# A GNN and FFN stack on one core: the products of the zero matrix in TensorE's waits are taken out

## The reference

```python
edge_index = jnp.stack([src, dst])                        # 8192 edges
x = x + L0_gnn(layernorm(x), edge_index, ...)             # GAT, 8 heads of 768, then GAT with one head
x = x + L0_ffn(layernorm(x)[None], ...)[0]                # class tokens, 5 atoms, gates
x = x + L1_gnn(layernorm(x), ..., edge_index)             # the same GAT again
x = x + L1_ffn(layernorm(x)[None], ...)[0]                # 768 -> 512 -> 768 -> 768
x = x + L2_gnn(layernorm(x), edge_index, W, b)            # GCN
x = x + L2_ffn(layernorm(x)[None], ...)[0]                # 8 experts of 64, the best one
x = x + L3_gnn(layernorm(x), edge_index, edge_type, ...)  # 34 relations, then GCN
x = x + L3_ffn(layernorm(x)[None], ...)[0]                # 8 experts of 96, the best two, layer norm
```

## Time and profile before

| | |
|---|---|
| median of three runs | 1344.08 us |
| the profiled execution's own time | 1338.48 us |
| its span, first to last instruction | 1336.7 us |
| TensorE busy | 1272.1 us, 95% |
| TensorE's weight loads busy | 1131.4 us, 85% |
| VectorE busy | 994.8 us, 74% |
| ScalarE busy | 643.2 us, 48% |
| mean granted clock of TensorE | 0.995 |

### The profile page before, as it was taken

How to read it: one execution, slowest core, us unless ns; L and a number is a source line. 1 busy time by engine, 2 the same in 40 slices (tenths; PEclk the granted TensorE clock), 3 DMA queues, 4 the chain that set the end, 5 groups by cost and what they waited for, 6 DMA issues and landing times.

```text
span 1336.7 us, 20982 instructions
## 1 busy us (share of the span) xinstructions
PE 1272.1 (95%) x7760; PEld 1131.4 (85%) x7778; DVE 994.8 (74%) x1639; ACT 643.2 (48%) x835; POOL 198.3 (15%) x160
## 2 busy tenths in 40 slices
PE   6999999988899999988898999999999999999997
PEld 4788999965888999967677889888888988888886
DVE  6998888987798888986867666655666665566676
ACT  5666566545566566545345433333443333343342
POOL 0023443430024443430000000000000000000200
PEclk9999999999999999999999999999999999999999
DMA  9495666654445666544245444554444454443640
GB/s 336 161 269 174 180 208 201 176 145 125 147 172 173 186 208 195 182 117 143 87 166 184 177 157 168 190 186 162 157 157 159 185 185 177 157 157 142 203 119 31
DMA packets 103929, 227.40 MB, mean 170 GB/s; under 512 B 16759, under 2 KB 34999, under 8 KB 103889
## 3 DMA queue, kind: packets, MB, share of 16 engines
q1 hardware_dynamic: 72972, 192.43, 40.6%
q10 hardware_dynamic: 20980, 31.78, 8.5%
q0 software_dynamic: 9936, 2.66, 2.2%
HBM read 216.56 MB, written 10.29 MB: 170 GB/s over the span
## 4 chain that ended last, share of the span: by engine, by line
PE 79%; DVE 12%; ACT 3%; DMA 3%; issue 2%; DVEq 0%; ACTq 0%; SPq 0%
PE bank L445 78%; DVE w_lo L1369 3%; DMA w_in<-L_gnn_W 2%; ACT w_hi L1011 1%; DVE stats L1407 1%; PE bank L541 1%; DVE h_lo L1369 1%; PE bank L484 1%; DMA w_in<-L_gnn_W_root 1%; DMA x_sb<-x 1%; DVE neg_b L1372 0%; DVE hid_lo L1369 0%; DVE x_sb L1369 0%; DVE xT_lo L1369 0%; DVE scores_b L1375 0%
## 5 line engine op out<-in xcount | busy, mean ns | idle before, releaser
L1011 ACT ACTIVATE w_hi<-w_in 128x2304 fp32r<-128x2304 f32 (+4 forms) x162 | 328.9, 2063 | 233.2 <-PE bank L445 198.7
L1369 DVE TENSOR_TENSOR w_lo<-w_in,w_hi 128x2304 fp32r<-128x2304 f32 (+4 forms) x162 | 396.6, 2477 | 58.3 <-ACT w_hi L1011 58.2
L445 PE MATMUL bank<-w_hi,xT_hi 128*128 128x384 f32 (+3 forms) x942 | 322.9, 343 | 6.2 <-DVE xT_lo L1369 4.2
L445 PE MATMUL bank<-w_lo,xT_hi 128*128 128x384 f32 (+3 forms) x942 | 306.2, 337 | 0.0
L445 PE MATMUL bank<-w_hi,hid_hi 128*128 128x512 f32 (+3 forms) x858 | 293.8, 342 | 7.6 <-DVE hid_lo L1369 4.4
L445 PE MATMUL bank<-w_lo,hid_hi 128*128 128x512 f32 (+3 forms) x858 | 271.3, 337 | 0.0
L445 PE MATMUL bank<-w_hi,xT_lo 128*128 128x384 f32 (+3 forms) x942 | 244.9, 338 | 0.0
L445 PE MATMUL bank<-w_hi,hid_lo 128*128 128x512 f32 (+3 forms) x858 | 224.9, 338 | 0.0
L445 PEld LDWEIGHTS bank<-w_hi,xT_hi 128*128 128x128 f32 (+1 forms) x942 | 176.4, 187 | 32.6 <-issue 5.7
L445 PEld LDWEIGHTS bank<-w_hi,hid_hi 128*128 128x128 f32 (+1 forms) x858 | 161.5, 188 | 44.5 <-issue 5.9
L1945 DVE SCALAR_TENSOR_TENSOR neg_b<-bank,rinv,neg_b 128x512 f32<-128x512 f32 (+1 forms) x136 | 77.4, 611 | 153.3 <-PE bank L445 153.3
(11 more groups left out here) (253 smaller groups left out, 1509.4 us busy)
## 6 DMA issues: line engine op xcount, KB each, us to landing
w_in<-L_gnn_W_rel SPq DMA_DIRECT2D x68, 1152.0 KB, 5.6
w_in<-L_gnn_W SPq DMA_DIRECT2D x66, 1152.0 KB, 5.7
table<-zrow SPq DMA_DIRECT2D x4, 2304.0 KB, 16.4
scores_b<-table ACTq DMA_DIRECT2D x34, 256.0 KB, 2.9
a_bc<-L_gnn_a_src ACTq DMA_DIRECT2D x18, 384.0 KB, 3.8
a_bc<-L_gnn_a_dst ACTq DMA_DIRECT2D x18, 384.0 KB, 5.3
key_row<-key_rows ACTq DMA_DIRECT2D x16, 256.0 KB, 5.5
w_in<-ffn_out SPq DMA_DIRECT2D x4, 864.0 KB, 6.0
```

The source lines that it names most:

```text
L445: return pe.matmul(out, lhsT, rhs, start=start, stop=stop, **kw)
L1011: act.activation(out, ps, func, **kw).then_inc(mark, 1)
L1369: return dve.tensor_tensor(out, a, b, op)
```

## The change

All `idle` calls are taken out, with the helper, the counts of `turn_tile` and `gcn`, and the eight products in `down_last`. The waits, semaphores, banks and all other work stay as they are.

```diff
-            def idle(b, n):
-                for _ in range(n):
-                    mm(bank[b][:, :], zero[:, 0:P], zero[:, :])
-            def turn_tile(i, m, n=0):
-                idle(TURNED[i][m][0], n)
+            def turn_tile(i, m):
                 pe.wait_ge(ln_xn, 2 * i + m + 1)
...
                 def down_last(h, n):
-                    for _ in range(8):
-                        mm(bank[1][:, :], zero[:, 0:P], zero[:, :], False, False, skip_group_check=True)
                     weights(n)
...
                 spread(9 * layer)
-                if layer == 0:
-                    idle(6, 3)
                 up_second(second[before_spread:before_turn])
                 turn(9 * layer)
                 up_second(second[before_turn:before_sum])
-                if layer == 0:
-                    idle(2, 3)
                 parts_kept(9 * layer)
...
                 down_last(HEADS - 1, n0 + 2 * HEADS)
-                idle(4, 4)
                 spread(HEADS + 9 * layer)
...
-                idle(3, 18 if layer == 0 else 20)
                 pe.wait_ge(h_high, (HEADS + 9 * layer) * 4 + 4)
                 turn(HEADS + 9 * layer)
...
-            turn_tile(1, 0, 4)
-            idle(4, 2)
+            turn_tile(1, 0)
             chunk(C_FFN0)
...
-            idle(0, 8)
             pe.wait_ge(f_dve[0], 7)
...
-            turn_tile(2, 0, 9)
-            idle(2, 2)
+            turn_tile(2, 0)
             gat(1)
...
-            turn_tile(3, 0, 4)
-            idle(2, 5)
+            turn_tile(3, 0)
             turn_tile(3, 1)
...
                 for sm in range(M):
-                    idle(fill, n[sm])
...
-            gcn(0, C_GCN2, 4, (8, 14), 4)
+            gcn(0, C_GCN2, 4)
...
             for m in range(M):
-                idle(2, 4 if m else 0)
                 pe.wait_ge(f_dve[2], 2 + m)
...
-            turn_tile(5, 0, 3)
-            idle(4, 2)
+            turn_tile(5, 0)
...
             mean(0, 0)
-            idle(7, 7)
             with pe.Fori(0, REL // 2 - 1) as i:
...
-            gcn(1, C_GCN3, 6, (6, 0), 3)
+            gcn(1, C_GCN3, 6)
...
-            idle(4, 8)
             for m in range(M):
                 pe.wait_ge(f_dve[3], 4 + m)
```

More of the change, by code:

```diff
@@ L809, in _, with gcn @@
             nodes(1, NODE_BANKS, node_tile(xT_hi, xT_lo, 1, K), of_w(0)).then_inc(w_used, 1)
-            def gcn(s, c, i, n, fill):
+            def gcn(s, c, i):
                 pe.wait_ge(e_cntT_low, 1)
```

## The result

The changed kernel takes 1356.55 us (median of 4 runs, 1356.30 to 1361.11), the kernel before 1344.44 us (4 runs). The ratio is 1.0103, with a 95% interval of 1.0084 to 1.0123. The same kernel run once more, beside 23 runs of the kernel before, gave 1.0093 [1.0078, 1.0108]. So it is 12 us, about 1%, slower. The profiled execution took 1356.36 us, span 1354.5 us, mean granted clock 0.971 against 0.995.

The account below looks back on a forecast made before the run. TensorE's own pace, and what stops it, was taken to bound the kernel. Clock-fall terms 6.5 + 1.4 + 3.1 + 0.7 + 1.1 - 0.3 = 12.5 us, added to the median 1344.08 us, gave 1356 us, range 1347 to 1363 us.

Parts of the forecast that it names:

- The products' own time: Almost nothing: 0.3 us gained at `idle(7, 7)` before the relation loop; 0.65 us at `idle(6, 3)` costed at 0.
- The price of a fall: Each clock fall with dense work behind it costs 1.7 us; its two ends are 0 and 3.4 us.
- The four sure waits: Waits at 654.53, 609.37, 711.10 and 331.96 sure to fall: three at 1.7 us, 331.96 at 1.4 us, together 6.5 us.
- The open waits: 1267.92: chance 0.8, 1.4 us; 276.69, its twin 576.94, 309.15: 0.6 each, 3.1 us; 321.83: 0.4, 0.7 us.
- The places that fell before: Before 303.14, its layer 1 twin, and 1310.27: fall already paid; short work inside runs slow, 1.1 us together.
- The covered waits: Waits at 649.22, 699.59 and 58.10: cost 0; up to 1.7 us each if the cover were gone.
- The mean clock: TensorE's mean granted clock would go from 0.995 to about 0.98.
- The median against the profiled execution: The 12.5 us sum was added to the median, 1344.08 us, which lay 5.6 us above the profiled execution.
- the losses are hidden: Rival, chance 0.10: ScalarE, VectorE or weights set the pace behind each wait; time within 2 us of 1344.
- faster: Rival, chance 0.04: real work starts earlier where filling reached the wait's end, 2.1 us in all, 1342 us.
- The clock holds in the doubtful waits: Rival, chance 0.15: waits of 2.4 to 3 us too short for a fall; sum 7.3 us, 1351 us.
- falls that last: Rival, chance 0.11: clock may stay down over two stretches, covered waits may not be covered; 21 us, 1365 us.

Follow-up runs that it names:

- 3: Kernel before with all 154 zero products kept, but 16 columns wide in place of 512: 1357.28 us, 1.0098.
- 4: Kernel before with three fp32 transposes for two zero products in every wait but `down_last`: 1345.17 us, 1.0002.
- 5: Kernel before with more zero products where its clock still fell (near 304, 604 and 1311 us): 1340.07 us, 0.9972.
- 8: Kernel before with the additions of 5 and more zero products in nearly every other wait: 1338.13 us, 0.9959.
- 11: Kernel before with every count of zero products halved, 74 in place of 154: 1353.95 us, 1.0080.
- 1: Changed kernel with zero products left in the four waits at 331.96, 609.37, 654.53 and 711.10 us: 1348.88 us, 1.0036.
- 2: Kernel before without only the 39 zero products of the waits at 331.96, 609.37, 654.53 and 711.10 us: 1348.40 us, 1.0032.
- 7: Kernel before without the 36 zero products of the covered places and of the wait at 331.96 us: 1343.33 us, 0.9997.
- 6: Kernel before without 47 zero products, those of waits behind which nothing was lost in the changed kernel, both `down_last` included: 1347.62 us, 1.0021.

## Why the prediction was right, and where it was not

It said 1356 us, ratio 1.009, by falls of the granted clock; 1356.55 us and 1.0103 were measured. That the loss comes from the clock in the waits is shown: the same instructions without the time they fill do not help (3), another filling does (4), more products than before help (5, 8), fewer help less (11), and the number of products by itself does not set the cost (1, 2, 7). That the number came within 1 us is luck in part. Against the profiled execution the changed kernel's trace lost 17.8 us where the sum had 12.5 us; that it was too small by 5 us was made up for by 5.6 us that the profiled execution of before was ahead of its median. Term by term, in us of the profiled executions:

- *The products' own time.* The gain of 0.3 us before the relation loop did not come. In the changed kernel the last `hid_lo` and the product behind it (VectorE, then TensorE with two other rows of the changed kernel that are used below):

```profile
746.38 2.06 DVE L1346 TENSOR_TENSOR hid_lo<-bank,hid_hi 128x512 fp32r<-128x512 f32 x3
```

```profile
302.38 1.08 PE L535 MATMUL bank<-ident,alpha 128*128 128x128 f32 x4 [5.42 <-DVE alpha L1349]
...
748.77 0.49 PE L445 MATMUL bank<-w_hi,hid_hi 128*128 128x512 f32 x1 [1.70 <-DVE hid_lo L1346]
...
1326.46 2.49 PE L936 MATMUL bank<-ident,spare 128*97 128x128 f32 x16 [3.75 <-DVE spare L1346]
```

`hid_lo` ends at 746.38 + 2.06 = 748.44 us and the product starts 0.33 us later, where the earlier trace rows had 0.34 us. So this time is there without the zero products too; the reading that they held the product up was wrong. At `idle(6, 3)` the work behind does start some 0.6 us earlier without them, and the next wait, for `alpha`, takes it back, so the cost of 0 was right. That wait in the kernel before and in the changed kernel:

```profile
58.10 0.66 PE L541 MATMUL bank<-ident,alpha 128*128 128x128 f32 x4 [0.99 <-DVE alpha L1372]
...
58.04 0.66 PE L535 MATMUL bank<-ident,alpha 128*128 128x128 f32 x4 [1.62 <-DVE alpha L1349]
```

- *The price of a fall, 1.7 us.* Right at 324 to 334 (1.5 us), 652 to 682 (1.5 us) and, in the first run, 1271 to 1310 us (1.5 us; 2.5 us repeated). Behind the longest waits the low stretch was twice as long or more, and 611 to 652 us cost 2.6 us, 716 to 734 us 2.8 and 1.4 us: towards the 3.4 us that the prediction kept as the upper end of one fall.
- *The four sure waits, 6.5 us.* 331.96 cost nothing instead of 1.4 us. The step that failed is the cover: I counted the 0.26 us that TensorE waits for `w_lo` at 340.49, and not the 1.73 us that it waits for `scal` at 354.62 nor VectorE's 1.20 us for weights ahead of that (experiment 7). This is the sign of being wrong that the prediction named, a fall with the next wait shorter by the same amount, at one of the four. The other three cost 2.6 + 1.5 + 2.8 = 6.9 us where I had 5.1 us (5.5 us repeated); these errors cancel.
- *The open waits.* 1267.92: right. 321.83, given 0.4: fell in both executions, 1.5 us. 276.69, its twin, and 309.15, given 0.6 each: none fell in either, 3.1 us too much. In other kernels they did fall: 276.69 in experiment 1, its twin in 1 and 6, and 309.15 in 11. Weighing them by a chance was right, and the price of the three is a difference between executions.
- *The places that fell before, 1.1 us.* Mis-sized the most: 1.6 and 1.2 us around 303 and 603 us, and 1.7 us (2.6 us repeated) from 1310 us on, 4.5 us in all. I had asked only what runs slow inside the wait. The clock went down early in the wait (0.65 over 293.83 to 304.95) and stayed down longer behind it: 0.59 over the 24 products, where they had 0.72 in the kernel before. The four transposes took 1.08 us, not 0.63 us, a little more than the 0.3 us that I put on them. The sixteen gained in the first run, 2.49 us for 3.12 us, and the loss came behind them; in the repeated run they took 0.6 us more, near the 0.5 us that I put on them:

```profile
1327.36 3.73 PE L936 MATMUL bank<-ident,spare 128*97 128x128 f32 x16 [3.73 <-DVE spare L1346]
```

- *The covered waits.* 58.10 and 649.22: nothing lost, as said. In the repeated run the clock did fall behind 58.10, 1.3 us were lost by 62 us, and at 80 us, behind the transfer of weights, nothing of it was left. 699.59: 0.7 us lost from 682 to 702 us in one execution, 0.2 us in the other.
- *What was not foreseen.* The 1.5 us of the transfer before 110 us, and 1.2 us from 380 to 409 us in both executions, in a stretch that has no zero product: a wait of 1.86 us for `w_lo`, which the kernel before has too, was followed by a fall here and in experiments 1, 2, 4 and 11, and not in the others. Why is open.
- *The mean clock.* About 0.98 was forecast, 0.971 was measured: more of the span was at 1.2 GHz than the sum of the falls had it.
- *The median against the profiled execution.* Adding the sum to the median came out, but the 5.6 us between the two, which I left unexplained, are by the mean clocks (0.991 and 0.995) in large part the same mechanism: falls that the other runs had and that one had not. The sum, read from that execution, probably counts some falls anew that the median had already.

Of the rivals, "the losses are hidden" holds at one of the places and not for the whole, and "faster" is refuted: the one place where a removed product had been in the way gave its 0.6 us back at the next wait. "The clock holds in the doubtful waits" and "falls that last" each describe a part: three doubtful waits held, and several falls lasted.

## What to carry to other kernels

Before costing filler work, or its removal, go wait by wait: how long TensorE is idle in all, whether the next engine's wait behind it is shorter than what a slow stretch loses, and only then sum. Fill up to the end of the wait and a little under: each product too many costs its own length, 0.22 us here, against 1.7 us for one fall; the counts of the kernel before still left 6 us in places that they filled only in part. Take the clock over several runs rather than from one profile, since the falls differ between executions of the same kernel.

## What the runs showed of the hardware

- With the waits filled by 16-column products the mean granted clock was 0.971 and the time 1.0098, as with empty waits; with products of 512 columns it was 0.991, and with fp32 transposes 0.988 and 1.0002. Data of zeros kept it up.
- Products of zeros themselves ran at half speed once the clock was down (0.40 us for 0.22 us in experiment 11).
- A kernel that leaves its arithmetic as it is, and adds only products that nobody reads, is 0.41% faster than the kernel before, which already had 154 of them (0.9959 [0.9946, 0.9972]).
- From one run to the next the same kernel had mean clocks of 0.987 to 0.994, and its times, 1340.83 to 1348.03 us, went along.
